# FFN down products of an attention + FFN block in three bf16 passes instead of one f32 product

## The chip, the cores and the metric

The kernel runs on one core of a Trainium2 chip. The metric is the device time of one execution in microseconds (us).

## What is computed

Two transformer layers with post-norm follow one another on 2048 tokens of width 256: attention with 16 heads and a gated FFN, then a retention layer and a mixture of experts. The change touches only the first FFN, whose weights are int8 with scales per column:

```python
x = _layernorm(x + _L0_attn_ref(x, ...), axis=-1)
x = _layernorm(x + _L0_ffn_ref(x, ...), axis=-1)

def _L0_ffn_ref(x, w_gate, w_up, w_down, s_gate, s_up, s_down):
    def _qmatmul(x, w_int8, scale):
        y = jnp.einsum('bsh,ho->bso', x, w_int8.astype(x.dtype))
        return y * scale
    gate = jax.nn.silu(_qmatmul(x, w_gate, s_gate))
    up = _qmatmul(x, w_up, s_up)
    fuse = gate * up
    return _qmatmul(fuse, w_down, s_down)
```

The hidden width of the FFN is 1024.

## The kernel before, in words

The program is a row of stages (attention, attention output with the first FFN, retention, routing, experts, combination). Each stage opens a block in which every engine has its own list of instructions, and all engines meet at a barrier between two stages. The stage of the change is `out_ffn`, from line 662. There TensorE is PE, VectorE is DVE, ScalarE is ACT, GpSimd is Pool. Nothing plans the order: each engine runs its list as written and waits on counting semaphores.

The 2048 tokens go in four chunks (c = 0 to 3) of 512. The hidden width goes in eight blocks (m = 0 to 7) of 128, and n = 8c + m numbers the 32 pairs. For each n:

- PE (`up`, line 752) makes the gate half g(n) and the up half u(n), each four f16 matmuls of 128x512 into one PSUM bank (line 761). There are two banks of each kind. g(n) waits until the silu of n-2 has read its bank, u(n) until the product of n-2 has read its bank.
- ACT (line 814) takes silu(n) of g(n) into `gate`.
- DVE (line 890) makes product(n) = u(n) x scale x gate into one slice of `fused[c % 2]`, f32. The second `fused` buffer is the old `pv_t` of the attention, so the profile calls it `l0b_pv_t`.

After the eight blocks of chunk c, PE runs `down(c-1)` (line 764), the down products of the chunk before: for each of its four token tiles eight f32 products, weights = a 128x128 piece of `fused`, moving = `w_down[:, m]` of 256 columns (line 771). So PE's order is up(0), up(1), down(0), up(2), down(1), turn(0), up(3), down(2), turn(1), down(3), turn(2), turn(3), where a turn (`norm_turn`, line 651) transposes a finished chunk for the next stage.

Two layernorms share the stage. The `first` one closes the attention and feeds the FFN. Its chunks 2 and 3, with the attention's output products (line 750), are worked into chunk 0 of the FFN. The other (`norm`) closes the FFN. In both DVE measures (lines 620 to 625), Pool takes the root of the variance (`norm_root`, line 632), and DVE waits for that root in `norm_scale` (line 640) before anything later in its list. DVE's list: after product 3 it measures `first` chunk 2, after product 4 it scales it, after product 5 it measures chunk 3, after product 6 it scales it. Ahead of product 4 of every chunk but the last, DVE splits the next chunk of x in two f16 parts (`split_x`, lines 847, 849 and 852). After the products of chunk c it runs `close(c-1)`: four scaled additions (lines 859 and 612), measure, wait for the root, scale. Pool's list before has, after the last of the attention's sums, only the roots: first 2, first 3, norm 0 to 3.

At the start of the stage ACT turns the int8 down weights into `w_down` in f32 (line 805).

Of the kernel before, what the change touches and what calls it, by code (L numbers as in the profile page):

```python
# [7 lines left out]
BF16 = mybir.dt.bfloat16  # L8
# [4 lines left out]
ALU = mybir.AluOpType  # L13
ACT = mybir.ActivationFunctionType
AX = mybir.AxisListType

P = 128
BATCH, SEQ, E = 2, 1024, 256
# [3 lines left out]
CH = 512  # L22
NCH = TOK // CH
# [9 lines left out]
PARTS = 3  # L33
# [534 lines left out]
MT = INTER // P  # L568
LAG = 1
TC = CH // P  # L570
# [5 lines left out]
F_REST = 6 * PARTS * CH // 2  # L576
# [52 lines left out]
def norm_root(pool, norm, c):  # L629

    pool.wait_ge(norm["var_in"], c + 1)
    pool.tensor_tensor(norm["rstd"][:, c * TC:(c + 1) * TC], norm["var"][:, c * TC:(c + 1) * TC],  # L632
                       norm["half"][:, 0:TC], ALU.pow).then_inc(norm["rstd_in"], 1)
# [29 lines left out]
def out_ffn(nc, a, keep):  # L663

    with ExitStack() as ctx:
        sb, ps, sem = scope(nc, ctx, "ffn0")
        x_t, o_tok = keep["x_t"], keep["o_tok"]
        f = front_views(keep["front"])
        w_out, w_up, s_up, s_down = (f[n] for n in ("w_out", "w_up", "s_up", "s_down"))
        w_down = sb("w_down", [P, MT, E])  # L670
        prod, pv_t, coef, total = (keep[n] for n in ("prod", "pv_t", "coef", "total"))
        QB = CH // 32
        o_t = [sb(f"o_t{i}", [P, KT, CH]) for i in range(2)]
        x_parts = [sb(f"x_parts{i}", [P, HALVES, KT, CH], F16) for i in range(2)]
        x_rest = sb("x_rest", [P, KT, CH])
        gate = [sb(f"gate{i}", [P, CH]) for i in range(2)]
        fused = [sb("fused0", [P, MT, CH])[:],
                 pv_t[:].rearrange("p k n d -> p (k n d)").rearrange("p (m n) -> p m n", m=MT)]
        y_sb = [sb(f"y_sb{i}", [P, E]) for i in range(2)]
        g_ps = [ps(f"g{i}") for i in range(2)]  # L680
        u_ps = [ps(f"u{i}") for i in range(2)]
# [34 lines left out]
        @block.gpsimd  # L716
        def _(pool):
            pool.tensor_tensor(prod[:], pv_t[:, :, :, 0:D0],
                               coef[:].rearrange("p n k -> p k n").unsqueeze(3)
                               .to_broadcast([P, KTS, QB, D0]), ALU.mult).then_inc(sum_chain, 1)  # L720
            pool.wait_ge(sum_chain, 1)
            pool.tensor_tensor(prod[:, 0:4], prod[:, 0:4], prod[:, 4:8], ALU.add).then_inc(sum_chain, 1)
            norm_root(pool, first, 0)
            pool.wait_ge(sum_chain, 2)
            pool.tensor_tensor(prod[:, 0:2], prod[:, 0:2], prod[:, 2:4], ALU.add).then_inc(sum_chain, 1)
            norm_root(pool, first, 1)
            pool.wait_ge(sum_chain, 3)
            pool.tensor_tensor(prod[:, 0], prod[:, 0], prod[:, 1], ALU.add).then_inc(sum_chain, 1)
            pool.wait_ge(sum_chain, 4)
            pool.tensor_tensor(o_tok[:, 2 * BATCH - 1, (QC - 1) * QB:QC * QB, D0:2 * D0], prod[:, 0],  # L730
                               total[:].unsqueeze(2).to_broadcast([P, QB, D0]), ALU.mult).then_inc(combined, 1)
            for c in range(2, NCH):
                norm_root(pool, first, c)
            for c in range(NCH):
                norm_root(pool, norm, c)

        @block.tensor
        def _(pe):
# [27 lines left out]
            def down(c):  # L766
                for t in range(c * TC, (c + 1) * TC):
                    bank = y_bank("down", t)
                    for m in range(MT):
                        pe.wait_ge(fuse, c * MT + m + 1)  # L770
                        mm = pe.matmul(bank[:, 0:E], fused[c % 2][:, m, t % TC * P:(t % TC + 1) * P], w_down[:, m],
                                       start=(m == 0), stop=(m == MT - 1))
                    mm.then_inc(made, 1)

            def turn_last(c):
# [26 lines left out]

        @block.scalar
        def _(act):
            act.activation(w_down[:], f["raw_down"], ACT.Copy).then_inc(cast, 1)
            norm_keep(act, first, 0)
            for c in range(NCH + 2):
                if c < NCH:
                    for m in range(MT):
                        n = c * MT + m  # L810
                        act.wait_ge(gated, n + 1)
                        if n >= 2:
                            act.wait_ge(fuse, n - 1)
                        act.activation(gate[n % 2][:], g_ps[n % 2][:], ACT.Silu,
                                       scale=s_up[:, 0, m:m + 1]).then_inc(silu, 1)
                        if c == 0 and m == 0:
                            norm_keep(act, first, 1)
                        if c == 1 and m in (0, 2):
                            norm_keep(act, first, 2 + m // 2)
                if c >= 2:  # L820
                    norm_keep(act, norm, c - 2)

        @block.vector
        def _(dve):
# [53 lines left out]
            for c in range(NCH + 1):  # L878
                if c < NCH:
                    for m in range(MT):  # L880
# [2 lines left out]
                            split_x(c + 1)  # L883
                        dve.wait_ge(upped, n + 1)
                        dve.wait_ge(silu, n + 1)
                        if c == 1 and m == 0:
                            dve.wait_ge(combined, 1)
                        if c >= 2:
                            dve.wait_ge(made, (c - 1) * TC)
                        dve.scalar_tensor_tensor(out=fused[c % 2][:, m], in0=u_ps[n % 2][:],  # L890
                                                 scalar=s_up[:, 1, m:m + 1], in1=gate[n % 2][:],
                                                 op0=ALU.mult, op1=ALU.mult).then_inc(fuse, 1)
                        if c == 0 and m == 1:
# [1055 lines left out]
```

## Time and profile before

| | us |
|---|---|
| median of 3 runs | 1465.17 |
| lowest and highest | 1461.19 and 1465.23 |
| time of the profiled execution | 1456.11 |
| its span | 1454.4 |

In the profile, busy times of an engine are sums of its instructions. Starts are us from the start of the span. An f32 matmul of the source with 256 moving columns appears as two MATMUL records, so the 32 f32 products of one `down` are 64 records; a bf16 or f16 matmul is one record, and so is an f32 transpose. A record of a matmul lasts longer than the spacing between two of them, since matmuls are pipelined; the spacing is read from the starts in the timeline.

### The profile page before, as it was taken

The page shows a single profiled execution, that of the slowest core. Times are in us where ns is not written, and L with a number is a line of the kernel's source. Part 1 is how long each engine was busy: PE and PEld are TensorE (multiplying, and loading weights), DVE is VectorE, ACT ScalarE, POOL GpSimd, SP SyncE. Part 2 cuts the span into 40 slices and gives each one's busy share as a digit, 9 for nine tenths or more (in the row PEclk, how much of TensorE's full clock was granted, in tenths as well). Part 3 has the DMA queues.
Part 4 walks back from the last instruction along what each step waited for, and adds up shares of the span by engine and source line. Part 5 has one row for each costly group of instructions (what it writes and reads, how often), then busy time and mean ns, then how long its engine had stood idle before and what let it go on. Part 6 is the DMA issues. An engine that isn't in the chain of part 4 may idle for free. (4 is left out here: it accounts for less than half of the span.)

```text
span 1454.4 us, 19589 instructions
## 1 busy us (share of the span) xinstructions
PE 1185.9 (82%) x6248; PEld 689.2 (47%) x6287; DVE 818.7 (56%) x1572; ACT 520.6 (36%) x1052; POOL 550.8 (38%) x564
## 2 busy tenths in 40 slices
PE   5589999999999699989997515699999997778641
PEld 2242222222222255665455511188888886664321
DVE  6499999999997565333446379712221221114554
ACT  1137777777778432101234100033333332221000
POOL 6002447663536500012110105454444443314775
PEclk9799999999999889989998755589999999888855
DMA  4960531443101400000000100199999999962343
GB/s 133 182 151 8 91 46 21 52 58 45 21 10 16 166 2 1 0 1 1 1 1 1 60 0 1 33 295 303 313 306 305 308 302 231 220 192 57 101 127 97
DMA packets 142584, 154.78 MB, mean 106 GB/s; under 512 B 50674, under 2 KB 111443, under 8 KB 142419
## 3 DMA queue, kind: packets, MB, share of 16 engines
q1 hardware_dynamic: 106882, 98.71, 26.9%
q0 software_dynamic: 12288, 33.57, 9.2%
q10 hardware_dynamic: 23312, 21.24, 4.5%
q8 instruction: 52, 0.85, 0.3%
q14 instruction: 50, 0.40, 0.1%
HBM read 118.34 MB, written 32.51 MB: 104 GB/s over the span
## 5 line engine op out<-in xcount | busy, mean ns | idle before, releaser
L495 ACT ACTIVATE l_ret_store<-attn_st 128x512 f32<-128x512 f32 x512 | 280.0, 598 | 103.5 <-PE attn_st L406 87.3
L519 DVE TENSOR_REDUCE attn_neg<-attn_mx 128x8 f32<-128x1024 f32 x256 | 299.1, 1202 | 13.0 <-PE attn_mx L386 12.1
L1713 DVE COPY exp_y_sb<-exp_y_ps 128x256 f32<-128x256 f32 x160 | 68.0, 425 | 288.7 <-PE exp_y_ps L1658 288.7
L1624 POOL DMA_INDIRECT exp_rows<-x_rows,moe_tok_i x160 | 150.9, 943 | 189.2 <-PE exp_xt_ps L1638 172.6
L1649 PE MATMUL exp_h_ps<-exp_xt,exp_w 128*88 128x128 f32 x1280 | 174.2, 281 | 23.2 <-DMA exp_w<-in_w 22.8
L386 PE MATMUL attn_mx<-attn_k_st,attn_q_st 96*128 96x512 bf16 x512 | 154.9, 384 | 17.8 <-DVE attn_neg L519 15.1
L1658 PE MATMUL exp_y_ps<-exp_w,exp_ht 96*128 96x256 f32 x640 | 167.9, 385 | 0.0
L1649 PEld LDWEIGHTS exp_h_ps<-exp_xt,exp_w 128*88 128x88 f32 x1280 | 150.3, 161 | 32.2 <-DMA exp_w<-in_w 31.1
L406 PE MATMUL attn_st<-attn_q_st,attn_k_st 128*128 128x512 bf16 x473 | 160.0, 383 | 5.3 <-ACT l_ret_store L495 2.3
L418 PE MATMUL attn_o<-l_ret_store,l_ret_tab 128*32 128x512 f32 x1024 | 136.4, 604 | 2.8 <-ACT l_ret_store L495 0.8
L1678 ACT ACTIVATE exp_xt<-exp_xt_ps 128x256 f32<-128x256 f32 x160 | 61.5, 384 | 210.4 <-PE exp_xt_ps L1638 206.8
L406 PEld LDWEIGHTS attn_st<-attn_q_st,attn_k_st 128*128 128x128 bf16 x512 | 48.1, 97 | 157.2 <-ACT l_ret_store L495 114.6
L1757 POOL DMA_INDIRECT comb_got<-y_rows,moe_slot_i x96 | 92.6, 965 | 78.3 <-POOLq L58 33.1
L1658 PEld LDWEIGHTS exp_y_ps<-exp_w,exp_ht 96*128 96x128 f32 x640 | 110.9, 193 | 9.2
L1685 ACT ACTIVATE exp_ht<-exp_h_ps 88x256 f32<-88x256 f32 x160 | 60.8, 380 | 114.6 <-PE exp_h_ps L1649 114.6
L278 POOL CAST attn_neg_parts<-attn_neg 128x128 bf16<-128x128 f32 x16 | 4.6, 290 | 209.1 <-DVE attn_neg L519 209.1
L386 PEld LDWEIGHTS attn_mx<-attn_k_st,attn_q_st 96*128 96x128 bf16 x512 | 48.5, 98 | 67.6 <-DVE attn_neg L519 29.5
L1822 DVE SCALAR_TENSOR_TENSOR keep_x<-comb_got,moe_weight,keep_x 128x256 f32<-128x256 f32 x96 | 46.6, 486 | 42.4 <-DMA comb_got<-y_rows,moe_slot_i 38.9
L1638 PE MATMUL exp_xt_ps<-keep_ident,exp_rows 128*128 128x128 f32 x320 | 63.1, 279 | 6.8 <-DVE exp_w L1708 6.0
L1490 PE MATMUL route_m<-route_hot_high,route_hot_low 128*128 128x320 bf16 x96 | 42.2, 447 | 26.8 <-DVE route_hot_high L1576 22.1
L354 PE MATMUL attn_st<-keep_x_t,l0b_front 128*128 128x512 f32 x64 | 37.1, 741 | 32.4 <-DVE l0b_front L505 25.1
L1783 PE MATMUL comb_y<-comb_w_down,comb_sh_h 128*128 128x256 f32 (+1 forms) x96 | 33.8, 510 | 35.4 <-DVE keep_x L612 35.4
(233 smaller groups left out, 1643.9 us busy)
## 6 DMA issues: line engine op xcount, KB each, us to landing
exp_w<-in_w SPq DMA_DIRECT2D x320, 176.0 KB
y_rows<-exp_y_sb ACTq DMA_DIRECT2D x160, 128.0 KB, 6.2
parts<-l0b_front SPq DMA_DIRECT2D x32, 192.0 KB, 11.3
attn_k_st<-parts SPq DMA_DIRECT2D x48, 128.0 KB, 7.2
attn_q_st<-parts SPq DMA_DIRECT2D x48, 128.0 KB, 7.9
l_ret_tab<-in_tables SPq DMA_DIRECT2D x4, 1024.0 KB
exp_rows<-x_rows,moe_tok_i POOLq DMA_INDIRECT x160, 6.3
keep_x_t<-in_x_t SPq DMA_DIRECT2D x4, 512.0 KB
```

The lines of the kernel that those rows point to most:

```text
L386: mm = pe.matmul(bank[:, half * CH:(half + 1) * CH], q, k_st[g % BUFS][0:STACK, h, half * CH:(half + 1) * CH], start=True, stop=True)
L406: pe.matmul(st_ps[n % BANKS][:], k_st[g % BUFS][:, h, kt * P:(kt + 1) * P], q_st[g % BUFS][:, h, c * CH:(c + 1) * CH], start=True, stop=Tr ...
L418: mm = pe.matmul(o_ps[32 * h:32 * h + 32, :], v_st[:, b, kt, head + h], probs[s % 2][:, h], start=True, stop=True)
L495: act.activation(probs[s % 2][:, h], st_ps[n % BANKS][:], ACT.Exp, scale=SCALE0).then_inc(exp_done, 1)
L519: dve.tensor_reduce(neg[m % 2][:, i], mx_ps[slot["score", n] % 2][:].rearrange("p (j k) -> p j k", k=P), AX.X, ALU.max, negate=True).then_ ...
L1624: pool.indirect_dma_start(rows[b % RB][:], None, a["x_rows"], bass.IndirectOffsetOnAxis(ap=tok_i[:, b:b + 1], axis=0)).then_inc(rows_in[b ...
L1638: mm = pe.transpose(xt_ps[b % 2][:, k * P:(k + 1) * P], rows[b % RB][:, k * P:(k + 1) * P], ident[:])
L1649: mm = pe.matmul(h_ps[b % 2][0:HALF, j * P:(j + 1) * P], w1[n][:, k, j], xt[b % 2][:, k], start=(k == 0), stop=(k == KT - 1))
L1658: mm = pe.matmul(y_ps[b % 2][:, 0:E], ht[b % 2][:, j], w2[b % B][:, j], start=(j == 0), stop=(j == 1))
L1678: act.activation(xt[b % 2][:], xt_ps[b % 2][:, 0:KT * P].rearrange("p (k t) -> p k t", k=KT), ACT.Copy).then_inc(xt_in, 1)
L1713: dve.tensor_copy(y_sb[b % YB][:], y_ps[b % 2][:, 0:E]).then_inc(y_in, 1)
L1757: pool.indirect_dma_start(got[n % B][:], None, a["y_rows"], bass.IndirectOffsetOnAxis(ap=slot_i[:, t, k:k + 1], axis=0)).then_inc(got_in[n ...
```

## The change

`fused` becomes three bf16 buffers for each of the two chunks. DVE writes product(n) in f32 to a ring of three `stage` buffers. ACT copies it to bf16 (high), Pool subtracts high from it into one of two f32 `left` buffers, ACT copies `left` to bf16 (mid), Pool subtracts mid from `left` into bf16 (low). PE then runs three bf16 matmuls where there was one f32 product. `w_down` is bf16; int8 values fit it. The buffers lie in memory that the attention and the raw weights have left.

The lists change with it. ACT: silu(n), high(n-1), mid(n-2). Pool: high subtraction of n, low subtraction of n-1, and the roots in between: first 2 after n = 4, first 3 after n = 6, norm 0 after n = 15, norm 1 after n = 23, norm 2 and 3 at the end. Product(n) waits for the high subtraction of n-3.

```diff
@@ -667,15 +667,20 @@
         x_t, o_tok = keep["x_t"], keep["o_tok"]
         f = front_views(keep["front"])
         w_out, w_up, s_up, s_down = (f[n] for n in ("w_out", "w_up", "s_up", "s_down"))
-        w_down = sb("w_down", [P, MT, E])
+        w_down = sb("w_down", [P, MT, E], BF16)
         prod, pv_t, coef, total = (keep[n] for n in ("prod", "pv_t", "coef", "total"))
         QB = CH // 32
         o_t = [sb(f"o_t{i}", [P, KT, CH]) for i in range(2)]
         x_parts = [sb(f"x_parts{i}", [P, HALVES, KT, CH], F16) for i in range(2)]
         x_rest = sb("x_rest", [P, KT, CH])
         gate = [sb(f"gate{i}", [P, CH]) for i in range(2)]
-        fused = [sb("fused0", [P, MT, CH])[:],
-                 pv_t[:].rearrange("p k n d -> p (k n d)").rearrange("p (m n) -> p m n", m=MT)]
+        spare = [keep["front"][:, F_REST + i * CH:F_REST + (i + 1) * CH] for i in range(4)]
+        stage, left = spare[0:3], [spare[3], sb("left1", [P, CH])[:]]
+        two = pv_t[:].rearrange("p k n d -> p (k n d)").bitcast(BF16).rearrange("p (a m n) -> p a m n", a=2, m=MT)
+        one = prod[:].rearrange("p k n d -> p (k n d)").bitcast(BF16).rearrange("p (m n) -> p m n", m=MT)
+        fused = [[sb(f"fused0_{i}", [P, MT, CH], BF16)[:] for i in range(PARTS)], [two[:, 0], two[:, 1], one]]
+        high_in, left_in, mid_in, low_in = (sem(n) for n in ("high_in", "left_in", "mid_in", "low_in"))
+        NM = NCH * MT
         y_sb = [sb(f"y_sb{i}", [P, E]) for i in range(2)]
         g_ps = [ps(f"g{i}") for i in range(2)]
         u_ps = [ps(f"u{i}") for i in range(2)]
@@ -729,9 +734,32 @@
             pool.wait_ge(sum_chain, 4)
             pool.tensor_tensor(o_tok[:, 2 * BATCH - 1, (QC - 1) * QB:QC * QB, D0:2 * D0], prod[:, 0],
                                total[:].unsqueeze(2).to_broadcast([P, QB, D0]), ALU.mult).then_inc(combined, 1)
-            for c in range(2, NCH):
-                norm_root(pool, first, c)
-            for c in range(NCH):
+
+            def take_high(n):
+                pool.wait_ge(high_in, n + 1)
+                if n >= 2:
+                    pool.wait_ge(low_in, n - 1)
+                pool.tensor_tensor(left[n % 2], stage[n % 3], fused[n // MT % 2][0][:, n % MT], ALU.subtract
+                                   ).then_inc(left_in, 1)
+
+            def take_mid(n):
+                c = n // MT
+                pool.wait_ge(mid_in, n + 1)
+                if c >= 2 and n % MT == 0:
+                    pool.wait_ge(made, (c - 1) * TC)
+                pool.tensor_tensor(fused[c % 2][2][:, n % MT], left[n % 2], fused[c % 2][1][:, n % MT],
+                                   ALU.subtract).then_inc(low_in, 1)
+
+            for n in range(NM):
+                take_high(n)
+                if n >= 1:
+                    take_mid(n - 1)
+                if n in (4, 6):
+                    norm_root(pool, first, n // 2)
+                if n % MT == MT - 1 and MT < n < NM - 1:
+                    norm_root(pool, norm, n // MT - 1)
+            take_mid(NM - 1)
+            for c in range(NCH - 2, NCH):
                 norm_root(pool, norm, c)
 
         @block.tensor
@@ -767,9 +795,10 @@
                 for t in range(c * TC, (c + 1) * TC):
                     bank = y_bank("down", t)
                     for m in range(MT):
-                        pe.wait_ge(fuse, c * MT + m + 1)
-                        mm = pe.matmul(bank[:, 0:E], fused[c % 2][:, m, t % TC * P:(t % TC + 1) * P], w_down[:, m],
-                                       start=(m == 0), stop=(m == MT - 1))
+                        pe.wait_ge(low_in, c * MT + m + 1)
+                        for p in range(PARTS):
+                            mm = pe.matmul(bank[:, 0:E], fused[c % 2][p][:, m, t % TC * P:(t % TC + 1) * P], w_down[:, m],
+                                           start=(m == 0 and p == 0), stop=(m == MT - 1 and p == PARTS - 1))
                     mm.then_inc(made, 1)
 
             def turn_last(c):
@@ -802,6 +831,19 @@
 
         @block.scalar
         def _(act):
+            def high(n):
+                c = n // MT
+                act.wait_ge(fuse, n + 1)
+                if c == 1 and n % MT == 0:
+                    act.wait_ge(combined, 1)
+                if c >= 2 and n % MT == 0:
+                    act.wait_ge(made, (c - 1) * TC)
+                act.activation(fused[c % 2][0][:, n % MT], stage[n % 3], ACT.Copy).then_inc(high_in, 1)
+
+            def mid(n):
+                act.wait_ge(left_in, n + 1)
+                act.activation(fused[n // MT % 2][1][:, n % MT], left[n % 2], ACT.Copy).then_inc(mid_in, 1)
+
             act.activation(w_down[:], f["raw_down"], ACT.Copy).then_inc(cast, 1)
             norm_keep(act, first, 0)
             for c in range(NCH + 2):
@@ -813,6 +855,14 @@
                             act.wait_ge(fuse, n - 1)
                         act.activation(gate[n % 2][:], g_ps[n % 2][:], ACT.Silu,
                                        scale=s_up[:, 0, m:m + 1]).then_inc(silu, 1)
+                        if n >= 1:
+                            high(n - 1)
+                        if n >= 2:
+                            mid(n - 2)
+                        if n == NM - 1:
+                            high(n)
+                            mid(n - 1)
+                            mid(n)
                         if c == 0 and m == 0:
                             norm_keep(act, first, 1)
                         if c == 1 and m in (0, 2):
@@ -883,11 +933,11 @@
                             split_x(c + 1)
                         dve.wait_ge(upped, n + 1)
                         dve.wait_ge(silu, n + 1)
-                        if c == 1 and m == 0:
-                            dve.wait_ge(combined, 1)
-                        if c >= 2:
-                            dve.wait_ge(made, (c - 1) * TC)
-                        dve.scalar_tensor_tensor(out=fused[c % 2][:, m], in0=u_ps[n % 2][:],
+                        if n == 0:
+                            dve.wait_ge(cast, 1)
+                        if n >= 3:
+                            dve.wait_ge(left_in, n - 2)
+                        dve.scalar_tensor_tensor(out=stage[n % 3], in0=u_ps[n % 2][:],
                                                  scalar=s_up[:, 1, m:m + 1], in1=gate[n % 2][:],
                                                  op0=ALU.mult, op1=ALU.mult).then_inc(fuse, 1)
                         if c == 0 and m == 1:
```

## Rows read from the trace of the kernel before

**Rows 1.** The page: span, TensorE's busy time, granted clock in 40 slices.

```profile
span 1454.4 us, 19589 instructions
...
PE 1185.9 (82%) x6248; PEld 689.2 (47%) x6287; DVE 818.7 (56%) x1572; ACT 520.6 (36%) x1052; POOL 550.8 (38%) x564
...
PEclk9799999999999889989998755589999999888855
```

**Rows 2.** Windows: PE, PEld, DVE, ACT, POOL busy, clock, DMA; down(0), then up(2).

```profile
552.20:565.90 13.70, 13.70 (x65) 12.07 (x64) 3.30 (x7) 0.03 (x1) 0.00 (x0) 1.00 0.00 0
566.01:581.62 15.61, 13.99 (x65) 6.25 (x64) 11.40 (x25) 5.47 (x8) 1.01 (x1) 1.00 0.01 2
```

**Rows 3.** Timeline of TensorE: start, length, line, names, shapes, count, [idle before].

```profile
552.20 13.98 PE L771 MATMUL ffn_y<-ffn_w_down,ffn_fused 128*128 128x256 f32 x64
566.01 1.03 PE L761 MATMUL ffn_g<-ffn_x_parts,l0b_front 128*128 128x512 f16 x4
...
572.12 1.04 PE L761 MATMUL ffn_u<-ffn_x_parts,l0b_front 128*128 128x512 f16 x4 [1.62 <-DVE ffn_fused L890]
...
595.44 1.04 PE L651 MATMUL ffn_turn<-keep_ident,keep_x 128*128 128x128 f32 x8
...
601.54 1.04 PE L761 MATMUL ffn_u<-ffn_x_parts,l0b_front 128*128 128x512 f16 x4 [0.75 <-DVE l0b_pv_t L890]
```

**Rows 4.** Groups of instructions on Pool, shapes apart: busy us, mean ns.

```profile
L1030 POOL TENSOR_TENSOR ret_qk_t<-ret_cos_part,ret_sin_part 128x512 f32<-128x512 f32 x16 | 20.3, 1268 | 72.2 <-DVE ret_sin_part L1231 72.2
...
L284 POOL TENSOR_TENSOR attn_neg_parts<-attn_neg_rest,attn_neg_parts 128x128 bf16<-128x128 f32 x16 | 6.8, 427 | 1.3
L280 POOL TENSOR_TENSOR attn_neg_rest<-attn_neg,attn_neg_parts 128x128 f32<-128x128 f32 x16 | 6.8, 427 | 1.3
```

**Rows 5.** Groups of instructions on ScalarE, shapes apart.

```profile
L814 ACT ACTIVATE ffn_gate<-ffn_g,l0b_front 128x512 f32<-128x512 f32 x32 | 22.0, 688 | 58.8 <-PE ffn_g L761 54.4 <-DVE ffn_fused L890 2.7 <-DVE l0b_pv_t L890 1.8
L463 ACT ACTIVATE l0b_front<-attn_st 128x512 bf16<-128x512 f32 x16 | 9.6, 597 | 57.9 <-PE attn_st L354 32.8 <-DMA parts<-l0b_front 25.1
...
L1213 ACT ACTIVATE ret_soft<-ret_soft 128x1024 f32<-128x1024 f32 x4 | 4.2, 1052 | 0.0
```

**Rows 6.** Timeline of chunk 0 and before it: DVE and Pool on shared moments.

```profile
506.91 0.72 POOL L728 TENSOR_TENSOR l0b_prod<-l0b_prod 128x256 f32<-128x256 f32 x1
506.98 0.81 DVE L640 TENSOR_SCALAR keep_x<-keep_x,ffn_first_ln_mv,ffn_first_ln_rstd 128x256 f32<-128x256 f32 x1
...
527.58 0.69 DVE L847 TENSOR_SCALAR ffn_x_parts<-keep_x_t 128x1024 f16<-128x1024 f32 x1
527.75 1.39 POOL L632 TENSOR_TENSOR ffn_first_ln_rstd<-ffn_first_ln_var,keep_neg_half 128x4 f32<-128x4 f32 x1 [19.41 <-DVE ffn_first_ln_var L625]
```

**Rows 7.** Timeline of VectorE in chunk 0: products 4, 5 and 7.

```profile
530.17 0.74 DVE L890 SCALAR_TENSOR_TENSOR ffn_fused<-ffn_u,l0b_front,ffn_gate 128x512 f32<-128x512 f32 x1
...
532.78 0.74 DVE L890 SCALAR_TENSOR_TENSOR ffn_fused<-ffn_u,l0b_front,ffn_gate 128x512 f32<-128x512 f32 x1
...
538.40 0.74 DVE L890 SCALAR_TENSOR_TENSOR ffn_fused<-ffn_u,l0b_front,ffn_gate 128x512 f32<-128x512 f32 x1
```

**Rows 8.** Timeline in up(2): root of norm 0, its scaling, products 16 and 17.

```profile
568.98 1.01 POOL L632 TENSOR_TENSOR ffn_ln_rstd<-ffn_ln_var,keep_neg_half 128x4 f32<-128x4 f32 x1 [31.91 <-DVE ffn_ln_var L625]
570.02 1.38 DVE L640 TENSOR_SCALAR keep_x<-keep_x,ffn_ln_mv,ffn_ln_rstd 128x256 f32<-128x256 f32 x4 [1.12 <-POOL ffn_ln_rstd L632]
571.32 1.40 DVE L890 SCALAR_TENSOR_TENSOR ffn_fused<-ffn_u,l0b_front,ffn_gate 128x512 f32<-128x512 f32 x2
```

**Rows 9.** Timeline of TensorE after idle times; PEld is its weight load.

```profile
511.77 1.89 PE L761 MATMUL ffn_g<-ffn_x_parts,l0b_front 128*128 128x512 f16 x4 [7.24 <-DVE ffn_x_parts L852]
...
644.12 1.94 PE L651 MATMUL ffn_turn<-keep_ident,keep_x 128*128 128x128 f32 x8 [3.53 <-DVE keep_x L640]
...
652.08 0.33 PEld L1052 LDWEIGHTS ret_a<-keep_x_t,l_ret_store 128*128 128x128 f32 x1 [0.52 <-issue]
652.91 0.19 PEld L1052 LDWEIGHTS ret_a<-keep_x_t,l_ret_store 128*128 128x128 f32 x1 [0.50 <-issue]
```

## Prediction

> **What bounds the kernel now.** I read the page first. It gives the span, and TensorE as the busiest engine at 82% [rows 1]; its granted clock has dips, which matter below. The chain that ended last says nothing of this change, for it stays in the last stage. The stages are parted by a barrier, so whatever the first FFN's stage gains or loses goes into the total one for one, and the question is what sets the end of that stage. The windows answer it: in down(0) TensorE is busy for the whole 13.70 us and Pool not at all; in up(2), 15.61 us long, TensorE is busy for 13.99, and DVE, ACT and Pool have 11.40, 5.47 and 1.01 [rows 2]. So TensorE sets the pace, but for small stalls which its timeline names: 1.62 us in up(2) and 0.75 us in up(3), both waiting for a product of DVE [rows 3]. The last 3.53 us before the last turn are a layernorm's latency [rows 9].
>
> **Part 1, fewer passes.** From the starts, one down is 64 records in 13.81 us (552.20 to 566.01), 216 ns each [rows 3]. After, it is 96 bf16 matmuls of 256 columns. None stands in the trace. From above: no f32 record of 256 columns took more than 216 ns. From below: f16 matmuls of 512 columns with a new weight each are 216 ns apart (four in 0.86 us), half of which is 108; and the eight f32 transposes that start at 595.44, each with a fresh weight, took 0.87 us, again 108 ns each, so a load is hidden at that spacing [rows 3]. I take 108 and keep 160 (halfway to 216) for a rival. 96 x 0.108 = 10.4 us, 3.4 less per down, four times: **-13.7 us**.
>
> **Part 2, the new work.** Per n, Pool gets two subtractions of 128x512. The f32 one takes 1268 ns; at 128x128 a bf16 and an f32 output both take 427, so I take 1.27 for both (ends: 0.8 and 1.4) [rows 4]. With waits that is 2.6 us per n, where TensorE needs 1.73 for up(n) (eight f16 matmuls) and, with down, 24.2 per chunk against Pool's 20.8 plus roots. Pool keeps up on average; but inside an up it is the slower one. ACT gets two copies: 597 ns from PSUM to bf16, and half of 1052 plus overhead from SBUF, so 0.55 to 0.6. With the silu of 688 that is about 1.85 per n [rows 5], also more than 1.73. DVE's product keeps its size. The cast of `w_down` hides under DVE's and TensorE's first products of the stage, as before. No DMA moves.
>
> **Part 3, the roots behind the subtractions.** This is the costly part: Pool's queue was empty, so a root began at once, and DVE's scaling and all products after it hang on the root. I walk the list, with the gaps between engines as they are now.
> - Chunk 0. Product 4 starts at 530.17, product 5 at 532.78 [rows 7]. New: the split ahead of product 4 can wait for one Pool instruction (+1.2, see below), so product 4 ends near 532.1. Then high(4) 0.6, subtractions 4 and 3 2.5, root 1.0, scale 1.4, product 5 0.7: 538.4, 5 us late. Then additions and measure, product 6 at 541.6. The same row of five steps (0.6, 2.5, 1.0, 1.4, 0.7): product 7 ends at 547.9, where it ended at 539.1 [rows 7]. TensorE's u(9), which started at 540.1, has to wait for product 7: **+7.8**. Seen from TensorE these are stalls of 1.2 (second output product), 1.6 (u7), 1.4 (u8) and 3.6 (u9).
> - Up(1) from there. TensorE could do the rest in 12.1 us; ACT has backlog, two keeps and 1.85 per n, and the split before product 12 waits for Pool again: **+2.4** (ends 0 and 5).
> - Up(2), T its start. Norm root 0 stands behind subtraction 15, which waits for high(15), which ACT issues after silu(16). g(16) is there at T+1.0, silu T+1.7, high(15) T+2.3, subtractions 15 and 14 T+4.9, root T+5.9, scale T+7.3, product 16 T+8.0. Now product 16 ends at about T+6.0 (root at T+2.97) [rows 8]. The stall of 1.62 becomes 3.6: **+2.0**; Pool's and ACT's pace and the split add **+1.9**.
> - Up(3). The same chain, +3.0, since the turn ahead of it hides less than it does of 0.75 now, and +0.6 for ACT's pace: **+3.6**. There is no split in it.
> - The tail after down(3): Pool has long been done, the 3.53 us stay.
>
> Sum so far: -13.7 + 7.8 + 2.4 + 2.0 + 1.9 + 3.6 = **+4.0 us**.
>
> **Part 4, the port.** A scaling of DVE (normally 0.41) that began 0.07 after a Pool addition of 0.72 took 0.81, till just after the addition had ended; and a Pool root that began during DVE's tensor_scalar of `split_x` took 1.39 instead of 1.01 [rows 6, 8]. So these forms exclude each other. I have this for two of the three instructions of a split (lines 847 and 852), and it is in the terms above (1.2 us in chunk 0, about 1.3 in chunks 1 and 2). The scalings stay free, since Pool waits for the product behind them.
> The Trainium skill, SBUF — State Buffer, section "Who interferes with whom", goes further: a DVE instruction with two SBUF inputs contends with a GpSimd instruction that reads SBUF. That would take in the middle one of the split (line 849). No row here shows that form beside such a Pool instruction; it is rival A.
>
> **Part 5, the clock.** After an idle of 3.53 us TensorE's eight transposes took 1.94 instead of 1.04, and the loads stayed slow until near 652.5, after a second idle; after 7.24 us four matmuls took 1.89 instead of 1.03. After 1.62 us nothing changed [rows 3, 9]. The slow ones run at the lower of the two levels, 1.2 instead of 2.4 GHz. The new stalls of u9, u18 and u26 are 3.6 to 3.8 us each. If each is followed by 4 us at the lower level, as in [rows 9], each loses 2 us; ACT's pace hides about 1 of the 6: **+5** (ends: 0 if the clock holds, and 8).
> The Trainium skill, TensorE: Matmul & The Clock Gate, section "HAM oscillation — how this bites in real kernels", warns of just such idle gaps; by it too this term would not be nought. The rows agree at 3.53 us.
>
> **Sum: +9 us.** On the profiled execution, 1456.1 + 9 = 1465.1. That execution lies 9.1 below the median of the runs, 1465.17; carried over, the median after is **1474.2 us**.
>
> **Rivals.**
> - A, the port holds for the middle instruction of the split too. It then waits up to 1.3 us for a Pool subtraction, and the last one behind it for one more: 2.5 us in each of chunks 1 and 2 and 1.3 in chunk 0, 6.3, of which TensorE's idle time there already covers 1. The sum without the clock is +9.5, the stalls ahead of u14 and u22 grow to 3.5 to 4.4 us, two more than bring the lower clock, and with it the sum is +15 to +20: 1480 to 1485. This is the case that the rule of the Trainium skill in part 4 describes. For: nothing in [rows 6] speaks against; against: the root in [rows 6] seems to have run on beside line 849. Chance 0.20.
> - B, no change. The clock holds, since TensorE works up to each stall and right after, and DVE's splits slip between subtractions: the walk gives +1.2 to +4, 1466 to 1469. For: 1.62 us did no harm. Chance 0.20.
> - C, the other side: faster. Pool's subtraction with bf16 in or out is quicker than f32, 0.8 us; then root, scale and products come 1 us earlier at each of four places, Pool never sets the pace of up, and the gain of part 1 stays: -3 to -6, 1459 to 1462. It decides at about 1.0 us. Against: 427 at 128x128 for both outputs, little less than a line through the f32 rows would give [rows 4]. Chance 0.09.
> - D, the bf16 matmul of 256 columns with a fresh weight is 160 ns apart, as if the load were not hidden: down takes 15.4 instead of 13.8, and the sum is +29 with the stalls of part 3 and the clock, 1494. Against: the transposes [rows 3]. Chance 0.06.
>
> **Chances.** Forecast (+5 to +13) 0.45, A 0.20, B 0.20, C 0.09, D 0.06. A change of under 0.3%, 4.4 us, can't be told from none here. Slower: forecast, A and D, 0.71; same: B, 0.20; faster: C, 0.09. The range leaves out C, D and little else: 1465 to 1486.
>
> **What would show it.** In the changed profile: down of 96 matmuls in 10.4 us (15 would be D); L640 of `first` chunk 3 near 546 and of norm 0 about 6 us after up(2) starts; TensorE waiting for DVE products before u(9), u(18), u(26) by 3.6 to 3.8 us, with a granted clock under 1.00 in the windows behind them; Pool's subtractions at 1.27; split instructions of line 847 near 1.9 instead of 0.68, and under rival A line 849 longer than 1.3. I am wrong if the stalls are under 2 us or if down(0) starts before 558.

## The result, and the profile after

The changed kernel takes 1476.84 us (median of 6 runs, 1474.30 to 1480.53) against 1465.20 for the kernel before in the same comparison (6 runs, 1461.19 to 1480.38): a ratio of 1.0072, 95% interval 1.0044 to 1.0100. The forecast was 1474.2 us, slower. The profiled execution took 1477.09 us.

The page of the changed kernel (span, busy times, granted clock in 40 slices), to [rows 1]:

```profile
span 1475.0 us, 20047 instructions
...
PE 1189.7 (81%) x6415; PEld 681.7 (46%) x6415; DVE 827.9 (56%) x1572; ACT 553.4 (38%) x1116; POOL 628.8 (43%) x628
...
PEclk9789999999999888999998755589999999989765
```

Pool has 78 us more, ScalarE 33 us more. The page doesn't show where the time went; the stage's timeline does. I take the stage's length from the first attention-output matmul to the first matmul of the next stage: 156.6 us before (491.97 to 648.53), 169.2 after (493.57 to 662.74). These are the timeline's starts on TensorE:

| part | before | after | difference | forecast |
|---|---|---|---|---|
| up to up(0) | 19.80 | 20.19 | +0.4 | 0 |
| up(0) and up(1) | 40.43 | 55.70 | +15.3 | +10.2, and clock |
| up(2) | 15.61 | 21.91 | +6.3 | +3.9, and clock |
| up(3) | 14.74 | 18.93 | +4.2 | +3.6, and clock |
| four downs | 55.25 | 42.13 | -13.1 | -13.7 |
| turns and tail | 10.73 | 10.31 | -0.4 | 0 |
| sum | 156.6 | 169.2 | +12.6 | +9, of it +5 clock |

The two profiled spans differ by 20.6 us: 12.6 are the stage, 1.6 lie ahead of it and 6.4 behind it, in stages whose instructions the change leaves alone. The medians of the runs differ by 11.6, so I take that rest for scatter between executions and haven't followed it.

TensorE's timeline after, to [rows 3, 9]: the long stalls (in brackets) and the matmuls behind them, the output product, u(9), u(18) and u(26):

```profile
535.23 3.23 PE L778 MATMUL ffn_y<-l0b_front,ffn_o_t 128*128 128x256 f32 x8 [2.46 <-DVE keep_x L612]
...
550.61 1.89 PE L789 MATMUL ffn_u<-ffn_x_parts,l0b_front 128*128 128x512 f16 x4 [3.29 <-DVE l0b_front L940]
...
587.88 1.89 PE L789 MATMUL ffn_u<-ffn_x_parts,l0b_front 128*128 128x512 f16 x4 [3.23 <-DVE l0b_front L940]
...
621.24 1.89 PE L789 MATMUL ffn_u<-ffn_x_parts,l0b_front 128*128 128x512 f16 x4 [3.34 <-DVE l0b_front L940]
```

L940 is the product (L890 before). The stalls ahead of u(9), u(18) and u(26) are 3.29, 3.23 and 3.34 us, where the forecast had 3.6 to 3.8. Four matmuls behind each take 1.89 us in place of 1.03. Behind the shorter stall of u(14) the clock falls too, but one group of four later:

```profile
565.40 1.04 PE L789 MATMUL ffn_u<-ffn_x_parts,l0b_front 128*128 128x512 f16 x4 [2.34 <-DVE l0b_front L940]
566.27 1.68 PE L789 MATMUL ffn_g<-ffn_x_parts,l0b_front 128*128 128x512 f16 x4
567.75 1.91 PE L789 MATMUL ffn_u<-ffn_x_parts,l0b_front 128*128 128x512 f16 x4
569.46 10.87 PE L800 MATMUL ffn_y<-ffn_w_down,ffn_fused 128*128 128x256 bf16 x96
```

The windows show what clock that is; the columns are those of [rows 2]: behind the stall of u(9), behind that of u(14), in down(0), behind that of u(18):

```profile
550.00:556.00 6.00, 5.39 (x14) 2.16 (x15) 2.01 (x4) 5.38 (x10) 4.38 (x4) 0.50 0.01 3
...
566.40:569.40 3.00, 3.00 (x9) 1.01 (x7) 0.75 (x1) 2.83 (x6) 2.86 (x3) 0.52 0.00 0
...
569.67:580.16 10.49, 10.49 (x96) 9.36 (x95) 3.38 (x7) 0.63 (x1) 3.37 (x3) 0.99 0.01 2
...
587.00:592.00 5.00, 4.12 (x10) 1.50 (x11) 2.23 (x4) 3.25 (x6) 3.30 (x3) 0.50 0.01 2
```

A granted clock of 0.50 is the lower level, 1.2 GHz. A down at the full clock is 96 matmuls in 10.48 us (down(2), 632.35 to 642.83), 109 ns each; down(0) begins at the lower clock and takes 10.70.

The timeline after of VectorE and Pool around the split of chunk 1, to [rows 6]; L742 is the subtraction of high, L750 that of mid:

```profile
529.75 0.69 DVE L897 TENSOR_SCALAR ffn_x_parts<-keep_x_t 128x1024 f16<-128x1024 f32 x1
529.77 1.68 POOL L742 TENSOR_TENSOR ffn_left<-l0b_front,ffn_fused 128x512 f32<-128x512 f32 x1 [1.18 <-ACT ffn_fused L841]
530.47 2.06 DVE L899 SCALAR_TENSOR_TENSOR ffn_x_rest<-keep_x_t,ffn_x_parts 128x1024 f32<-128x1024 f32 x1
...
531.41 2.13 POOL L750 TENSOR_TENSOR ffn_fused<-l0b_front,ffn_fused 128x512 bf16<-128x512 f32 x1
...
532.56 1.53 DVE L902 TENSOR_SCALAR ffn_x_parts<-ffn_x_rest 128x1024 f16<-128x1024 f32 x1
```

Alone, L899 takes 1.22 us and L902 0.69; a subtraction takes 1.16. Here each of them contains a wait for the other engine: L902 ends at 534.09, after the subtraction that ended at 533.54. The first instruction of this split began just ahead of the subtraction and took its usual 0.69; those of the next two splits took 1.55 and 1.21. So all three instructions of a split and Pool's subtractions exclude one another, the middle one (two SBUF inputs) too.

The same view in up(2), to [rows 8]:

```profile
582.51 1.16 POOL L742 TENSOR_TENSOR ffn_left<-l0b_front,l0b_pv_t 128x512 f32<-128x512 f32 x1 [9.33 <-ACT l0b_pv_t L841]
...
583.62 1.16 POOL L750 TENSOR_TENSOR l0b_prod<-l0b_front,l0b_pv_t 128x512 bf16<-128x512 f32 x1
584.74 1.01 POOL L632 TENSOR_TENSOR ffn_ln_rstd<-ffn_ln_var,keep_neg_half 128x4 f32<-128x4 f32 x1
585.78 1.38 DVE L640 TENSOR_SCALAR keep_x<-keep_x,ffn_ln_mv,ffn_ln_rstd 128x256 f32<-128x256 f32 x4 [2.09 <-POOL ffn_ln_rstd L632]
587.08 1.40 DVE L940 SCALAR_TENSOR_TENSOR l0b_front<-ffn_u,l0b_front,ffn_gate 128x512 f32<-128x512 f32 x2
```

Up(2) starts at 580.16. The root comes at +4.6 and product 16 ends near +7.6 (forecast +4.9 and +8.0; before +3.0 and +6.0). Pool had waited 9.33 us for high(15), through most of down(0), and then did both subtractions ahead of the root.

### The profile page after: what moved, and what is told of

Its sections match the earlier page's. It is cut to its first block and busy times, and to the rows that moved or that the text cites. A ratio compares the mean times of both kernels' runs of the same rounds, so it can differ in the third digit from the quotient of the medians.

```text
span 1475.0 us, 20047 instructions
## 1 busy us (share of the span) xinstructions
PE 1189.7 (81%) x6415; PEld 681.7 (46%) x6415; DVE 827.9 (56%) x1572; ACT 553.4 (38%) x1116; POOL 628.8 (43%) x628
## 5 line engine op out<-in xcount | busy, mean ns | idle before, releaser
L519 DVE TENSOR_REDUCE attn_neg<-attn_mx 128x8 f32<-128x1024 f32 x256 | 299.0, 1200 | 13.8 <-PE attn_mx L386 12.8
L406 PE MATMUL attn_st<-attn_q_st,attn_k_st 128*128 128x512 bf16 x512 | 173.9, 384 | 4.0 <-ACT l_ret_store L495 2.1
L1833 PE MATMUL comb_y<-comb_w_down,comb_sh_h 128*128 128x256 f32 (+1 forms) x96 | 36.8, 545 | 46.1 <-DVE keep_x L612 26.7
L1102 PE MATMUL ret_a<-keep_x_t,l_ret_store 128*128 128x512 f32 x128 | 60.3, 625 | 2.1 <-PEq L58 2.1
```

Of the source, the lines that this page charges most:

```text
L406: pe.matmul(st_ps[n % BANKS][:], k_st[g % BUFS][:, h, kt * P:(kt + 1) * P], q_st[g % BUFS][:, h, c * CH:(c + 1) * CH], start=True, stop=Tr ...
L519: dve.tensor_reduce(neg[m % 2][:, i], mx_ps[slot["score", n] % 2][:].rearrange("p (j k) -> p j k", k=P), AX.X, ALU.max, negate=True).then_ ...
```

## The experiments

Three groups of kernels ran, each group on one chip with its own runs of the kernel before; ratios are to these. Three kernels were timed only once (experiments 2, 3 and 6); for them there is only the length of the stage. That repeats well: 169.2 and 169.0 us for the change, 157.9 and 158.3 for one of the variants, 162.3 and 162.2 for another. Where a stage is taken apart below, the parts are those of the table above.

**1. Only the passes.** The kernel before, with one bf16 product buffer that is multiplied three times.

```diff
-                        mm = pe.matmul(bank[:, 0:E], fused[c % 2][:, m, ...], w_down[:, m],
-                                       start=(m == 0), stop=(m == MT - 1))
+                        for p in range(PARTS):
+                            mm = pe.matmul(bank[:, 0:E], fused[c % 2][:, m, ...], w_down[:, m],
+                                           start=(m == 0 and p == 0), stop=(m == MT - 1 and p == PARTS - 1))
```

> On the kernel before: DVE writes each product in one bf16 buffer, TensorE multiplies that same buffer three times by bf16 weights; no high, mid or low parts are made, so ScalarE and Pool do what they did before. The parts left out are the splitting of the products. The stage's length is taken from the first attention-output matmul to the first matmul of the next stage: 156.6 us before, 169.2 after the change. Theory (passes save 13.7 us, all of the loss is the splitting's doing): stage near 143, kernel 13 to 14 us faster than before, 0.990 to 0.991. Rival (the bf16 passes bring less, for the loads aren't hidden, or TensorE's time is taken up by other waits): stage 150 or more.

Measured: ratio 0.9914 (0.9892 to 0.9936), 1439.27 against 1453.65 us; stage 142.8, 13.8 shorter. Its stalls are those of before, 0.80, 1.62, 0.75 and 3.53. Each down takes 10.48, so the passes bring 13.3 of the 13.8; the rest is mostly the turn behind the last layernorm, whose transposes took 1.32 here for 1.94. So the passes bring what was expected of them, and the change's splitting costs 26.4 us of stage.

**2. Roots earlier in Pool's list.**

```diff
             for n in range(NM):
+                if n % MT == MT - 1 and MT < n < NM - 1:
+                    norm_root(pool, norm, n // MT - 1)
                 take_high(n)
...
-                if n in (4, 6):
-                    norm_root(pool, first, n // 2)
-                if n % MT == MT - 1 and MT < n < NM - 1:
-                    norm_root(pool, norm, n // MT - 1)
+                if n in (3, 5):
+                    norm_root(pool, first, (n + 1) // 2)
```

> The changed kernel with Pool's four inner roots moved ahead: first 2 and 3 after n = 3 and 5, norm 0 and 1 ahead of the subtraction of n = 15 and 23. Theory queue alone (the roots stand behind subtractions, and nothing else matters): the stalls before u(9), u(18), u(26) go down to 1.6 us and less, stage 8 us shorter, near 161. Theory queue and port (a root that comes earlier sets off DVE's scalings beside Pool's subtractions, and each scaling then waits for one): the stalls stay at 3 to 4 us, stage 167 to 170, DVE's scalings take 0.8 to 1.5 us each in place of 0.41.

Measured: stage 157.9, 11.3 shorter. Timeline of this kernel at the start of up(2):

```profile
578.14 1.01 POOL L632 TENSOR_TENSOR ffn_ln_rstd<-ffn_ln_var,keep_neg_half 128x4 f32<-128x4 f32 x1 [7.38 <-DVE ffn_ln_var L625]
...
579.12 1.15 POOL L742 TENSOR_TENSOR ffn_left<-l0b_front,l0b_pv_t 128x512 f32<-128x512 f32 x1
579.18 3.04 DVE L640 TENSOR_SCALAR keep_x<-keep_x,ffn_ln_mv,ffn_ln_rstd 128x256 f32<-128x256 f32 x4 [1.12 <-POOL ffn_ln_rstd L632]
...
582.94 1.04 PE L789 MATMUL ffn_u<-ffn_x_parts,l0b_front 128*128 128x512 f16 x4 [3.28 <-DVE l0b_front L940]
```

The root is early, and four scalings take 3.04 us in place of 1.38, since they now meet Pool's subtractions: the stall ahead of u(18) stays at 3.28. That much is queue and port. But the stage is some 10 us shorter than that theory gave; both theories missed the size. Of the 11.3 us, 6.0 lie in up(0) and up(1): the stall of u(8) went, and those of u(9) and u(14) fell to 2.31 and 1.53. Up(2) and up(3) are 2.4 and 2.3 shorter, and in up(2) that is the clock's doing: behind 3.28 us of idle time the four matmuls took 1.04, the full clock. Behind the 2.31 us ahead of u(9) the clock did fall, again one group late. TensorE's timeline, then its windows:

```profile
549.20 1.04 PE L789 MATMUL ffn_u<-ffn_x_parts,l0b_front 128*128 128x512 f16 x4 [2.31 <-DVE l0b_front L940]
550.08 1.58 PE L789 MATMUL ffn_g<-ffn_x_parts,l0b_front 128*128 128x512 f16 x4
551.45 1.91 PE L789 MATMUL ffn_u<-ffn_x_parts,l0b_front 128*128 128x512 f16 x4
```

```profile
549.20:550.20 1.00, 1.00 (x5) 0.51 (x6) 0.60 (x1) 1.00 (x2) 0.31 (x1) 1.00 0.00 0
550.50:553.50 3.00, 3.00 (x9) 1.30 (x8) 0.75 (x1) 3.00 (x7) 2.68 (x3) 0.50 0.02 5
```

**3. Fillers.** 28 matmuls that nobody reads, where TensorE would stand idle.

```diff
                 for j, (bank, free, done) in enumerate(((g_ps, silu, gated), (u_ps, fuse, upped))):
+                    if j == 1 and n in (9, 18, 26):
+                        pe.wait_ge(*((first["summed"], NT) if c == 1 else (scaled, (c - 1) * TC)))
+                        for i in range(28):
+                            pe.matmul(y_ps[i % 2][:, E:2 * E], ident_bf[:], w_down[:, 0], start=True, stop=True)
...
+            pe.wait_ge(cast, 1)
             for t in range(2 * TC):
                 out(t)
```

> The changed kernel with 28 matmuls of 256 columns whose results nobody reads, placed ahead of u(9), u(18) and u(26), where TensorE stands idle for 3.2 to 3.3 us. They take 3.0 us at the full clock. Theory clock (the idle times bring the lower clock, which costs about 2 us behind each): no u or g matmul group of 1.9 us behind these places, granted clock 1.00 there, stage 3 to 6 us shorter, 163 to 166. Rival (ScalarE and Pool set the pace behind the stalls and hide the slow clock): stage within 1 us of 169.2.

Measured: stage 162.3, 6.9 shorter. The added wait for the cast makes the first output product start 0.6 us later (5.04 us of idle time ahead of it for 4.46), and the stage is counted from there; so 6.3 is the fillers' doing, 2.5 up to the end of down(0), 2.4 in up(2) and 1.4 in up(3). The timeline of TensorE in the later run of the same kernel shows a filled place and, in the same up(1), an unfilled one:

```profile
547.32 3.22 PE L788 MATMUL ffn_y<-ffn_w_down,keep_ident_bf 128*128 128x256 bf16 x28
550.78 1.04 PE L793 MATMUL ffn_u<-ffn_x_parts,l0b_front 128*128 128x512 f16 x4 [0.24 <-DVE l0b_front L945]
...
563.66 1.89 PE L793 MATMUL ffn_u<-ffn_x_parts,l0b_front 128*128 128x512 f16 x4 [3.19 <-DVE l0b_front L945]
```

Behind the fillers u(9) runs at 1.04. The stall ahead of u(14), 2.34 in the change, has grown to 3.19, and behind it u(14) runs at 1.89.

**4. A chunk's last parts at the chunk's end.** ScalarE and Pool no longer leave the parts of products 15 and 23 for the next chunk.

```diff
-                        if n >= 1:
+                        if n >= 1 and (c < 2 or m >= 1):
                             high(n - 1)
-                        if n >= 2:
+                        if n >= 2 and (c < 2 or m >= 2):
                             mid(n - 2)
-                        if n == NM - 1:
+                        if c >= 1 and m == MT - 1:
                             high(n)
...
+                if n % MT == MT - 1 and MT < n:
+                    take_mid(n)
+                    if n < NM - 1:
+                        norm_root(pool, norm, n // MT - 1)
```

> The changed kernel, but ScalarE and Pool finish the parts of a chunk's last product at the end of that chunk (from chunk 1 on), while TensorE does the down products, not behind the first silu of the next chunk. Roots norm 0 and 1 then stand behind nothing. Theory (the stalls of u(18) and u(26) come from high(15) being issued after silu(16), with two subtractions between it and the root): these stalls fall to 1.6 and 0.8 us as before, the lower clock behind them goes too, stage 8 to 10 us shorter, 159 to 161; kernel within 0.3% of the kernel before. Rival (Pool's pace sets the chunk anyway): stage 165 or more.

Measured: ratio 1.0024 (0.9995 to 1.0052), stage 157.9, 11.3 shorter. In up(2):

```profile
581.52 1.01 POOL L632 TENSOR_TENSOR ffn_ln_rstd<-ffn_ln_var,keep_neg_half 128x4 f32<-128x4 f32 x1 [4.85 <-DVE ffn_ln_var L625]
582.57 1.38 DVE L640 TENSOR_SCALAR keep_x<-keep_x,ffn_ln_mv,ffn_ln_rstd 128x256 f32<-128x256 f32 x4 [1.12 <-POOL ffn_ln_rstd L632]
...
584.66 1.04 PE L790 MATMUL ffn_u<-ffn_x_parts,l0b_front 128*128 128x512 f16 x4 [1.62 <-DVE l0b_front L941]
```

Pool waits for the variance again, as in [rows 8], and the stalls of u(18) and u(26) are 1.62 and 0.75, those of before. The theory holds: what made product 16 late was where the last high stood in ScalarE's list. Up(2) and up(3) are 4.2 us shorter each, 8.4 together, within the 8 to 10 expected. Of the rest, 2.4 lie in up(0), up(1) and down(0), where TensorE still waits for the same work in the same order; there only the clock differed (experiment 5).

**5. The change again.**

> The changed kernel as it is, once more, beside the others of this group on one chip. All theories: about 10 us slower than the kernel before, ratio 1.007. Theory clock (whether an idle time of 3.2 to 3.5 us brings the lower clock differs from one execution to the next, since chunk_end kept the full clock behind the same 3.29 us ahead of u(9) that lost it in the first profile): the 1.9 us groups may lie behind other stalls than u(9), u(18), u(26), and the stage is 162 to 170 us long. Rival (it is fixed by the length of the idle time): the same three places and 169 us.

Measured: ratio 1.0076 (1.0041 to 1.0110), stage 169.0; the stalls ahead of u(9), u(18) and u(26) are 3.28, 3.24 and 3.34, each with slow matmuls behind it. For this kernel the rival was right: the same three places, and the same two beside them, behind the output product (2.46) and u(14) (2.33). But across kernels the length of the idle time doesn't decide. TensorE's timeline of chunk_end, whose lists are the same up to the product of n = 15:

```profile
551.23 1.04 PE L790 MATMUL ffn_u<-ffn_x_parts,l0b_front 128*128 128x512 f16 x4 [3.29 <-DVE l0b_front L941]
...
564.13 1.89 PE L790 MATMUL ffn_u<-ffn_x_parts,l0b_front 128*128 128x512 f16 x4 [3.20 <-DVE l0b_front L941]
```

3.29 us left the clock as it was, 3.20 us a little later did not. The full clock behind u(9) also didn't bring all of its worth: the stall ahead of u(14) was 3.20 in place of 2.34. Up(0) and up(1) together took 53.50 us here, 55.70 and 55.63 in the two executions of the change.

**6. Splits inside the close.**

```diff
-                        if m == MT // 2 and c + 1 < NCH:
+                        if m == MT // 2 and c == 0:
                             split_x(c + 1)
...
                     norm_add(dve, norm, t, y_sb[t % 2][:])
+                    if t % TC == 1 and c + 2 < NCH:
+                        split_x(c + 2)
```

> The changed kernel with the splits of chunks 2 and 3 moved behind the second tile of close(0) and close(1), where TensorE runs a down and Pool mostly stands idle. Theory port (the splits ahead of products 12 and 20 take 4.8 us in place of 2.6 since each of their three instructions waits for a Pool subtraction, and Pool for them): their lengths go back to 0.68, 1.22 and 0.69, the stalls of u(14) and u(22), 2.3 and 1.6 us, go, stage 3 to 6 us shorter than as_changed. Rival (the stalls of u(14) and u(22) come from ScalarE's pace, 1.9 us per n): the stalls stay above 1 us.

Measured: stage 161.9, 7.1 shorter than experiment 5. The medians of the three instructions are 0.682, 1.226 and 0.694 us (0.94, 2.06 and 1.53 in experiment 5), and the stalls of u(14) and u(22), 2.33 and 1.62 us, are gone. The port theory holds; it gave 3 to 6. By the starts of the matmuls the two stalls had cost 2.5 and 1.8 us, 4.3 together; the rest is the clock, which no longer fell behind u(14) and stayed low for two groups behind u(18) where it had been for four. No stall is left in up(1) and up(2) but those of u(9) and u(18), so the rival, ScalarE's pace, is out.

**7. All three.** chunk_end, the moved splits, and the first layernorm's roots earlier.

> chunk_end and split_in_close together, and the first layernorm's roots of chunks 2 and 3 one place earlier in Pool's list (as in roots_first). Theory (late roots, port and clock are all of the loss): stage 149 to 153 us, 4 to 7 below the 156.6 of before; what is left of the loss lies in chunks 0 and 1, where Pool works beside the split and the scalings. Rival (Pool's and ScalarE's pace is a limit of its own): 155 or more.

Measured: ratio 0.9974 (0.9951 to 0.9997), stage 153.9. That is 0.9 above what was expected, and below the rival's: a stall of 2.31 remains ahead of u(9), with the lower clock from one group behind it, and most splits still met Pool (medians 1.16, 2.06 and 1.53 us), so that up(2) began 1.19 us late.

**8. Chunk 0 in f32.** chunk_end and the moved splits; the parts begin with n = 8, and down(0) uses f32 products and an f32 copy of the weights.

```diff
+                if n < MC:
+                    return
...
+                        if c == 0:
+                            pe.wait_ge(fuse, m + 1)
+                            mm = pe.matmul(bank[:, 0:E], whole[:, m, ...], w_down_f[:, m],
+                                           start=(m == 0), stop=(m == MT - 1))
+                            continue
```

> chunk_end and split_in_close, and chunk 0's down products in f32 as before (a second, f32 copy of the weights in the room of the attention's sums; chunk 1's low parts move to the room of the attention output's transposes). Chunk 0 then has no Pool work. Theory: the pass saving is 3 x 3.4 = 10.3 us, the losses of chunk 0 (stalls of the output product, u(7), u(8), u(9)) go, some 3 us of pace in chunk 1 stay: stage 148 to 150, kernel 6 to 8 us faster than before. Rival (chunk 1's ScalarE work, two keeps and 1.9 us per n, sets the pace of up(1)): stage 153 or more.

Measured: ratio 0.9943 (0.9923 to 0.9962), 1444.60 against 1453.49 us; stage 149.0. It beats both kernels. The stalls left are 0.80, 1.62, 0.71, 2.06 and the tail's.

**9. Three more.**

> The filler kernel once more, timed in rounds: the one look gave a stage of 162.3 us against 169.2 and 169.0 for the change itself. Theory clock (the fillers keep the full clock at three places): stage 161 to 165, ratio to the kernel before 1.001 to 1.005, against 1.0076 for as_changed. Rival (the one look was luck, the clock would have held anyway): ratio 1.006 to 1.009.

Measured: ratio 1.0061 (1.0032 to 1.0089), stage 162.2. The stage is what theory clock gave, the ratio what the rival gave. The stage, with the 0.6 us of the later start added, would make the ratio 1.0042; the interval holds that and experiment 5's 1.0076. The trace shows the full clock behind the fillers; the timing doesn't confirm it.

> roots_first once more, timed in rounds. Its stage of 157.9 us had no lower clock behind any stall, though the one ahead of u(18) was 3.28 us. Theory queue and port, with a clock that falls in some executions: stage 158 to 164, ratio 0.999 to 1.004. Theory that the early root is worth the full 11 us in every execution: 157 to 159, ratio 1.000 to 1.002.

Measured: ratio 1.0019 (0.9993 to 1.0045), stage 158.3, and again the full clock behind 3.19 and 3.29 us of idle time. Both ranges hold these numbers, so the run doesn't decide between them. It shows something else: here the clock did not fall behind the 2.31 us ahead of u(9), where it had fallen in roots_first, and yet up(0) and up(1) took 49.87 us against 49.73, since the stall ahead of u(14) was 3.19 in place of 1.53. The lower clock cost nothing there, since TensorE would have waited a little later anyway.

> mixed, with the two moved splits behind the third tile of the close, not the second: Pool has then ended its last subtractions. Theory port (in mixed the splits in close(1) still met Pool's last subtractions, 1.6, 2.1 and 1.5 us, and made up(3) wait 0.71 us): all splits at 0.68, 1.23 and 0.69 us, stage 147.5 to 149.5. Rival (a later split is later by more than it is shorter): stage 149.5 to 151.

Measured: ratio 0.9960 (0.9933 to 0.9987), stage 148.1. The middle and last instruction of all splits are at 1.23 and 0.69; one first instruction still met a subtraction (1.64). The stage is 0.9 shorter than that of mixed, which the ratio can't resolve.

## Why the prediction came out right, and what was off in it

- **Part 1, passes.** 10.4 us for a down, measured 10.5; -13.7, measured -13.3 in the downs of experiment 1. Spacing 109 ns for 108. Rival D is out.
- **Part 2, Pool's and ScalarE's times.** A subtraction takes 1.16 us, not 1.27; the f32 rows were a little dear for a bf16 input. A copy takes 0.62, a little over the 0.55 to 0.6. Rival C is out: Pool was not quick enough. The pace of the two engines, which the forecast had in three of its terms, cost nothing that shows (experiment 6).
- **Part 3, roots behind subtractions.** The mechanism was right, place by place. Stalls in the forecast 1.6, 1.4, 3.6 (u7, u8, u9), 3.6 (u18), 3.8 (u26); measured none, 1.36, 3.29, 3.23, 3.34. The one ahead of the output product, forecast at 1.2, was 2.46 for the 0.79 of before. Experiment 4 shows the mechanism for up(2) and up(3). There the better repair was not the one that the forecast pointed at: an earlier root alone runs into the port (up(2) 19.55 us), earlier highs don't (17.70).
- **Part 4, the port.** A step failed here: "I have this for two of the three instructions of a split". The middle one waits too, 2.06 us for 1.22. Rival A was right in its mechanism, and the rule of the Trainium skill (SBUF — State Buffer, "Who interferes with whom") that it stood beside agrees with the trace: an instruction of DVE with two SBUF inputs contends with a GpSimd instruction that reads SBUF. Yet the sum did not suffer, and that was luck. For pace and split together the forecast had +2.4 in up(1) and +1.9 in up(2); the stalls ahead of u(14) and u(22) cost 2.5 and 1.8 by the starts, all of it the splits' doing. A pace that cost nothing stood in for the wait that was left out. Rival A, which counted both, had stalls of 3.5 to 4.4 where 2.3 and 1.6 came, and +15 to +20 where 12.6 came (its own terms give +9.3 without the clock, not the +9.5 it states).
- **Part 5, the clock.** This is the term that was mis-sized. By the starts of the matmuls in up(0) to up(3), the stalls cost 15.1 us more than before, for a forecast of 17.7, and the lower clock 10.6 more, for a forecast of 5. Of the 10.6, 7.3 lie behind u(9), u(18) and u(26), of which the fillers gave back 6.3. Two places were missed: the 2.46 us ahead of the output product, behind which eight records took 3.23 us in place of 1.9 (1.7 in all), and the 2.34 us ahead of u(14) (1.5, and 0.2 in down(0)). Not all of the 10.6 can be had back, as roots_again shows.
- **Rival B, no change,** fell with both: the clock did not hold in the changed kernel, and no split slipped between subtractions.
- **The sum.** Stage +12.6 for +9, kernel +11.6 for +9.0, inside the range. The stalls came 2.6 under the forecast and the clock 5.6 over it, so part of the closeness is luck. What stays open is when an idle time of 2.3 to 3.3 us brings the lower clock.

## What to carry to other kernels

Before giving work to an engine that looks idle, list what short, urgent instructions stand in its queue and who waits for them: here a root of 1 us was behind 2.3 us of subtractions, which stood behind a copy that ScalarE issued one chunk late. Then look which instructions of VectorE would now run beside Pool's, since those with two SBUF inputs or a tensor_scalar wait for them. And an optimization need not cover the whole loop: with earlier highs and moved splits (and, in experiment 7, two earlier roots) the kernel was 0.3% faster than before when all chunks were changed, and 0.6% when the busiest one was left as it was.

## What the runs showed of the hardware that was not expected

- Idle times of TensorE of 3.19 to 3.35 us brought the lower clock in some places and not in others: behind 3.29, 3.23 and 3.34 in the change, not behind 3.29 in chunk_end, nor behind 3.28 in roots_first or 3.19 and 3.29 in roots_again. Shorter ones did it too: 2.46 us ahead of the output product in every kernel that had it, 2.34 ahead of u(14) in the change, and 2.31 ahead of u(9) in roots_first but not in roots_again.
- The fall need not come right behind the idle time. Behind the 2.34 and the 2.31 us the first four matmuls still took 1.04, and only the next ones 1.68 and 1.58 to 1.91 (clock 0.52 and 0.50), so looking only at the first group behind a stall misses it.
- A Pool instruction that loses the port is longer by its wait (a subtraction of 1.16 us took up to 2.13), so the cost doesn't appear as idle time on either engine.
- Even the DVE instruction of 0.17 us that adds EPS to 4 columns took 0.82 in up(2), where a subtraction had begun 0.36 us before it.
